# Two edge layers of a graph network: node degrees from the attention layer's ones column, eight row buffers, and PSUM for four and eight groups

## What is computed

```python
x = x + schnet(relu(layernorm(x)), src, dst, edge_weight, edge_attr)   # layer 0
x = x + gat(relu(layernorm(x)), src, dst)                              # layer 1, 8 heads
# layer 2: mean over neighbours
h   = relu(layernorm(x)) @ W + b
agg = segment_sum(h[dst], src);  deg = segment_sum(ones, src)
x   = x + agg * where(deg > 0, 1 / max(deg, 1), 0)[:, None]
# layer 3: two graph convolutions with batch norm; here loops are added once more
deg1 = segment_sum(ones, [dst, loops]);  dinv = rsqrt(deg1)
h = relu(batch_norm(segment_sum(dinv[s] * dinv[d] * (x @ W1)[s], d) + b1))   # 64 wide
z = batch_norm(segment_sum(dinv[s] * dinv[d] * (h @ W2)[s], d) + b2)         # 2 wide
x = x + z @ Wd + bd
```

## Time and profile before

| | |
|---|---|
| timed runs | 6829.5 us median of 3 (6825.88 to 6838.7) |
| profiled execution | 6840.93 us, span of the core 6839.2 us |
| PE / PEld busy | 4606.4 (67%) / 3811.0 us |
| DVE busy | 4114.3 us (60%) |
| POOL busy | 3517.6 us (51%) |
| ACT busy | 1523.6 us (22%) |
| mean granted clock of PE | 0.785 |

### The profile page before, as it was taken

One profiled execution on the slowest core, in us unless ns is written; L12 is line 12 of the kernel. 1 busy time (PEld: TensorE's weight loads), 2 busy tenths in 40 slices (PEclk: granted clock), 3 DMA queues, 4 the chain that ended last, 5 costly groups with the idle time before them and its releaser, 6 DMA issues. The chain is left out here.

```text
span 6839.2 us, 101942 instructions
## 1 busy us (share of the span) xinstructions
PE 4606.4 (67%) x25681; PEld 3811.0 (56%) x25681; DVE 4114.3 (60%) x11101; ACT 1523.6 (22%) x2509; POOL 3517.6 (51%) x3663
## 2 busy tenths in 40 slices
PE   4999999998957777777875666666663333333494
PEld 3777777776747777766764666666642222222231
DVE  3888888887646666666676555555553333333473
ACT  2666566554211111111122000000020000000272
POOL 1566666664055555555612666666615666666202
PEclk8999999999967877878877777777785555555596
DMA  4333333332333333333333222222232111111143
GB/s 146 105 91 90 89 90 90 91 90 75 108 86 84 83 79 81 83 79 82 85 90 119 85 85 85 85 85 86 86 91 47 22 22 22 22 22 22 35 114 106
DMA packets 417562, 537.32 MB, mean 79 GB/s; under 512 B 200349, under 2 KB 289577, under 8 KB 417353
## 3 DMA queue, kind: packets, MB, share of 16 engines
q0 software_dynamic: 154912, 381.74, 20.5%
q1 hardware_dynamic: 262442, 152.99, 8.4%
HBM read 482.43 MB, written 58.81 MB: 79 GB/s over the span
## 5 line engine op out<-in xcount | busy, mean ns | idle before, releaser
L489 POOL DMA_INDIRECT l_rows<-tmp_tab,l_idx x2496 | 2457.1, 984 | 1361.7 <-issue 712.7
L1919 PE MATMUL l_psa<-l_sel,l_rows 128*128 128x128 f32 (+1 forms) x4992 | 1093.5, 371 | 1314.5 <-DVE l_sel L507 1088.1
L1919 PEld LDWEIGHTS l_psa<-l_sel,l_rows 128*128 128x128 f32 (+1 forms) x4992 | 928.7, 244 | 1428.4 <-issue 803.7
L1886 DVE TENSOR_TENSOR acc<-acc,l_psa 128x256 f32 (+1 forms) x1664 | 584.0, 351 | 1193.1 <-issue 534.6
L1156 POOL DMA_INDIRECT l_rows<-tmp_tab,l_idx x832 | 866.7, 1042 | 586.6 <-PE l_psa L1470 329.7
L791 PE MATMUL l_psw<-l_fw,l_ssp 128*128 128x256 f32 x3328 | 782.4, 389 | 52.7 <-DVE l_msg L691 39.7
L791 PEld LDWEIGHTS l_psw<-l_fw,l_ssp 128*128 128x128 f32 x3328 | 624.7, 193 | 224.3 <-issue 73.2
L1470 PE MATMUL l_psa<-l_sel,l_rows 128*128 128x128 f32 x3328 | 627.2, 318 | 81.9 <-DVE acc L1358 43.2
L1358 DVE TENSOR_TENSOR acc<-acc,l_psa 128x384 f32 x832 | 460.8, 554 | 306.5 <-remote 96.2
L1470 PEld LDWEIGHTS l_psa<-l_sel,l_rows 128*128 128x128 f32 x3328 | 524.6, 224 | 106.1 <-DVE acc L1358 56.2
L507 DVE TENSOR_SCALAR l_sel<-iota,rel 128x128 f32<-128x128 f32 x1664 | 387.2, 295 | 193.7 <-issue 147.2
(11 more groups left out here) (313 smaller groups left out, 6243.3 us busy)
## 6 DMA issues: line engine op xcount, KB each, us to landing
l_rows<-tmp_tab,l_idx POOLq DMA_INDIRECT x3328
l_edge<-in_edge_t SPq DMA_DIRECT2D x104, 256.0 KB
tmp_x<-n_X SPq DMA_DIRECT2D x39, 512.0 KB
n_X<-in_x SPq DMA_DIRECT2D x26, 512.0 KB
tmp_tab<-n_O POOLq DMA_DIRECT2D x26, 512.0 KB
l_win<-tmp_att_tab SPq DMA_DIRECT2D x832, 8.0 KB
n_X<-tmp_x SPq DMA_DIRECT2D x26, 512.0 KB
l_lo_b<-tmp_lo_row SPq DMA_DIRECT2D x52, 256.0 KB
```

The costliest lines, as they stand in the source:

```text
L489: nc.gpsimd.indirect_dma_start(out=rows[b][:, t, :], out_offset=None, in_=table[:, :], in_offset=bass.IndirectOffsetOnAxis(ap=idx[q][:, j: ...
L1886: nc.vector.tensor_tensor(a, a, p, ALU.add).then_inc(added, 1)
L1919: last = nc.tensor.matmul(psa[0:n, col:col + P], rows[b][:, t, f:f + n], sel[b][:, t, :], start=True, stop=True)
```

## The change

The kernel after it differs in these places:

- l1: `wx` has a 17th column for each tile, which is one everywhere, so that row 16 of the third plane of `acc` counts the edges of each node. SP writes that row to memory at the start of n2.
- l2 and l3 have eight `rows` and `sel` buffers and four index buffers. PSUM holds `deep` groups, four in l2 and eight in l3, and DVE adds group g - LAG behind the selections of g, LAG being 3 and 7. PE and DVE loop over eight groups a turn, POOL over sixteen.
- l2: no ones product and no `deg` adds. ACT clears `acc`, DVE no longer. What n3 did first with the degrees stands here: the load at SP, the root at ACT, `degrees()` at DVE behind the third selection, and PE's products ahead of its loop, with the 64-wide copy of `dinv_c` replaced by a broadcast operand. The copies go to `dinv_r`, 64 partitions; `deg` is gone.
- n3 has only its staging, transposes and residuals.
- l3: the work for `split` stands behind the seventh selection, and the work after the loop ahead of the last seven adds.

```diff
@@ gather_all
         for b in range(NB):
+            r = (q * NB + b) % len(rows)
             hold(pool, ph, used, (it * NB + b) * per + per)
             if b == NB - 1 and more:
-                indices(it + 1, 1 - q)
+                indices(it + 1, (q + 1) % len(idx))
             for t in range(GT):
                 j = b * GT + t
                 nc.gpsimd.indirect_dma_start(
-                    out=rows[b][:, t, :], out_offset=None, in_=table[:, :],
+                    out=rows[r][:, t, :], out_offset=None, in_=table[:, :],
...
-    with pool.Fori(0, ITERS // 2 - 1) as pair:
-        for q in range(2):
-            tiles(pair * 2 + q, q, True)
+    with pool.Fori(0, ITERS // turns - 1) as turn:
+        for q in range(turns):
+            tiles(turn * turns + q, q, True)
@@ edges_gat
     W2 = 2 * HEADS
+    WC = W2 + 1
...
+                for w in wx:
+                    last = nc.vector.memset(by_edge(w)[:, :, W2:WC], 1.0)
...
-                            left = rows[c.r][:, j, k * P:(k + 1) * P] if k < KH else wx[c.p][:, j * W2:j * W2 + P]
+                            left = rows[c.r][:, j, k * P:(k + 1) * P] if k < KH else wx[c.p][:, j * WC:j * WC + P]
@@ nodes_gat, SP
+                sp.dma_start(dram["deg_row"][:, :], acc[W2:W2 + 1, KH, 0:NP]).then_inc(deg_out, 16)
@@ edges_rows
-def edges_rows(nc, dram, sh, tag, table, width, acc, count=None, split=None):
+def edges_rows(nc, dram, sh, tag, table, width, acc, deep, degree=None, split=None):
...
+    LAG = deep - 1
-        rows = [ph.sb(f"rows{i}", [P, GT, width]) for i in range(NB)]
-        idx = [ph.sb(f"idx{i}", [P, SEG], I32) for i in range(2)]
-        sel = [ph.sb(f"sel{i}", [P, GT, P]) for i in range(NB)]
+        rows = [ph.sb(f"rows{i}", [P, GT, width]) for i in range(ROWS)]
+        idx = [ph.sb(f"idx{i}", [P, SEG], I32) for i in range(4)]
+        sel = [ph.sb(f"sel{i}", [P, GT, P]) for i in range(ROWS)]
-        psa = ph.ps("psa", 2 * GT * wide)
-        psc = ph.ps("psc", 2 * GT * P)
+        psa = ph.ps("psa", deep * GT * wide)
...
+                @block.scalar
+                def _(act):
+                    for k in range(KH):
+                        last = nc.scalar.activation(acc[:, k, :], sh["iota"][:, 0:1].to_broadcast([P, NW]), ACT.Copy)
+                    last.then_inc(acc_zero, 1)
+                    act.wait_ge(deg_in, 16)
+                    nc.scalar.activation(dinv_c[:, :], deg_c[:, :], ACT.Sqrt, bias=sh["ones"][:, 0:1]).then_inc(rooted, 1)
+                    for c in range(CHUNKS):
+                        act.wait_ge(spread, c + 1)
+                        nc.scalar.activation(dinv_r[:, c * CN:(c + 1) * CN], psa[0:H3, (1 + c % 2) * CN:(2 + c % 2) * CN],
+                                             ACT.Copy).then_inc(roots, 1)
...
+                for b in range(ROWS):
+                    select(0, b)
+                    if b == LAG - 1:
+                        if degree:
+                            degrees()
+                        if split:
+                            bytes_of_sources()
+                    if b >= LAG:
+                        add(b - LAG, b - LAG)
+                with dve.Fori(1, GROUPS // ROWS) as turn:
+                    for b in range(ROWS):
+                        select(turn, b)
+                        add(turn * ROWS + (b - LAG), b - LAG + (ROWS if b < LAG else 0))
+                if split:
+                    same_destination()
+                for g in range(GROUPS - LAG, GROUPS):
+                    add(g, g % ROWS)
...
-                with pe.Fori(0, ITERS) as it:
-                    for b in range(NB):
+                with pe.Fori(0, GROUPS // ROWS) as turn:
+                    for b in range(ROWS):
...
-                            if count is not None:
-                                col = ((b % 2) * GT + t) * P
-                                last = nc.tensor.matmul(psc[:, col:col + P], sh["ones"][:, :], sel[b][:, t, :],
@@ bass_gnn_stack
-                    edges_rows(nc, dram, sh, "l2", dram["tab2"], D, acc, deg)
+                    edges_rows(nc, dram, sh, "l2", dram["tab2"], D, acc, 4, degree=(dinv_r, inv, last_edge, has, dinv_c))
-                edges_rows(nc, dram, sh, "l3", dram["tab3"], H3, acc3, split=(keep_on, one_dst, cont))
+                edges_rows(nc, dram, sh, "l3", dram["tab3"], H3, acc3, 8, split=(keep_on, one_dst, cont))
```

More of the change, by code:

```diff
@@ L1804, in edges_rows @@
             cleared_l, dst_in, linked = ph.sem("cleared_l"), ph.sem("dst_in"), ph.sem("linked")
-        psa = ph.ps("psa", 2 * GT * wide)
-        psc = ph.ps("psc", 2 * GT * P)
+        if degree:
+            dinv_r, inv, last_edge, has, dinv_c = degree
+            deg_c = ph.sb("deg_c", [P, NT])
+            upto, upper, ends = ph.sb("upto", [P, P]), ph.sb("upper", [P, NT]), ph.sb("ends", [P, NT])
+            deg_in, acc_zero, cols_done, cols_in = ph.sem("deg_in"), ph.sem("acc_zero"), ph.sem("cols_done"), ph.sem("cols_in")
+            counted, ranked, rooted, spread, roots = (ph.sem(n) for n in ("counted", "ranked", "rooted", "spread", "roots"))
+        psa = ph.ps("psa", deep * GT * wide)
         S = ph.sem
-        gathered = [S(f"gathered{i}") for i in range(NB)]
+        gathered = [S(f"gathered{i}") for i in range(ROWS)]
         idx_done, sel_done = S("idx_done"), S("sel_done")
-        cleared = S("cleared")
-        win_done = S("win_done", NB)
-        adds = 1 if count is None else 2
-        added = S("added", 2 * GT * adds)
+        win_done = S("win_done", ROWS)
+        added = S("added", deep * GT)
+        by_tile = lambda g: psa[:, g % deep * GT * wide:(g % deep + 1) * GT * wide].rearrange("p (t n) -> p t n", n=wide)
         ph.begin()
@@ L1842, in _ @@
                                              ).then_inc(dst_in, 16)
+            if degree:
+                @block.sync
+                def _(sp):
+                    with nc.allow_non_contiguous_dma(reason="one degree for each partition and node tile"):
+                        sp.dma_start(deg_c[:, :], dram["deg_row"].rearrange("a (t p) -> p (a t)", p=P)).then_inc(deg_in, 16)
+                    sp.wait_ge(deg_in, 16)
+                @block.scalar
[9 more added lines that the diff above has]
+                                             ACT.Copy).then_inc(roots, 1)
             @block.gpsimd
@@ L1862, in _, with same_destination @@
                     last.then_inc(cleared_l, 1)
[L1863 to L1898 removed]
+                def same_destination():
                     keep, one, cont = split
@@ L1913, in _ @@
+                with pe.Fori(0, GROUPS // ROWS) as turn:
+                    for b in range(ROWS):
+                        g = turn * ROWS + b
                         pe.wait_ge(sel_done, g + 1)
[L1914 to L1915 removed]
+                        pe.wait_ge(gathered[b], turn * 64 + 64)
+                        pe.wait_ge(added, GT * (g + 1))
                         for t in range(GT):
                             for k, (f, n) in enumerate(blocks):
[L1918 to L1923 removed]
+                                last = nc.tensor.matmul(by_tile(b)[0:n, t, k * P:(k + 1) * P], rows[b][:, t, f:f + n], sel[b][:, t, :],
@@ L1955, in _ @@
                 sp.dma_start(w[:, :, :], by_half(dram["gcn_w1"])).then_inc(w_in, 16)
-                sp.dma_start(dram["deg_row"][:, :], deg[0:1, 0:NP]).then_inc(deg_out, 16)
-                sp.wait_ge(deg_out, 16)
-                with nc.allow_non_contiguous_dma(reason="one degree for each partition and node tile"):
-                    sp.dma_start(deg_c[:, :], dram["deg_row"].rearrange("a (t p) -> p (a t)", p=P)).then_inc(deg_in, 16)
                 def step(at):
```

163 lines of the change are left out of this document (68 added, 95 removed).

## The result

The change makes the kernel a little faster: 6814.9 us median of 20 runs (6781.5 to 6830.4) against 6832.2 us for the kernel before in 20 runs of the same measurement, ratio 0.9966, 95% interval [0.9953, 0.9979]. By the ratio that is 23 us where 90 were forecast: the direction was right, and the size was not. The time lies outside the forecast's own range of 6700 to 6790, though inside the wide one of 6500 to 6820.

The account below looks back on a forecast made before the run. POOL's gathers, 5.03 us a group, were taken as the floor of l2 and l3, 1046 us each; -70 (l2) and -20 (n3) made -90, 6751 us, and 6740 as median of timed runs. Own range 6700 to 6790, wide range 6500 to 6820.

Parts of the forecast that it names:

- crawl: DVE in l3, some 8 us after POOL restarts: single adds 1.8 to 4.7 us apart, some 15 us a group.
- part (3): l2's start and end: POOL's 7 us wait goes, more groups are open at the last gather; net 0, -7 to +20.
- part (5): l3 with PSUM and buffers for eight groups, adds seven groups late: 0 us, bounds -25 and +25.
- part (2): l2 with more PSUM and buffers takes l3's pace, 5.89 us a group, 1225 us against 1294: -70 us.
- the ring: l2: DVE selects and adds for two groups, PE multiplies them; with PSUM for two, neither goes on before the other ends.
- Part (4): n3's prologue: only staging and the load of X stay, 7 us of 26.4: -20 us, or -12.
- Part (6): The ones column: stride 17 for 16, a fill at the attention layer's start, a row sent out during n2: 0 us.
- (A): Rival: l2's and l3's late signals are hidden by depth, both go to POOL's floor: -425, 6405 us; chance 0.22.
- (B): Rival: the longer DVE loop body in l2 and l3 costs a stop each turn of 8 groups: +92, 6921 us; chance 0.11.
- (C): Rival: l2 keeps its pauses and stays at 6.1 us a group, -25; in all -35, 6795 us; chance 0.13.
- (D): Rival: start and drain +20, l3 +25, l2 at -35: in all -10, 6820 us; chance 0.06.
- The rule of the skill: Instructions stream ahead in sequence, so only a taken branch leaving the two pages at hand, a loop's end, should starve DVE.

Follow-up runs that it names:

- e5: Kernel before, unchanged, on a chip with the crawl: to the last add, l2 took 1281 us and l3 1224 us.
- e6: Changed kernel, unchanged, on a chip with the crawl: ratio 0.9955 to the kernel before on that chip.
- e8: Changed kernel cut to the degree change alone (four buffers, PSUM for two groups), chip with the crawl: ratio 0.9940 to the kernel before.
- e1: Changed kernel cut to the degree change alone (four buffers, PSUM for two groups), chip without the crawl: ratio 0.9970 to the kernel before.
- e2: Changed kernel with l2's degree-chain copies over seven PSUM banks instead of two, chip without the crawl: ratio 0.9965 to the kernel before.
- f4: Changed kernel, unchanged, on a chip without the crawl: ratio 0.9958 to the kernel before on that chip.
- g1: Changed kernel with four row and selection buffers and PSUM for four groups in both layers, chip with the crawl: ratio 0.9908 to the kernel before.
- e11: Changed kernel with only one of l3's four gathers a group, chip with the crawl: l3 took 579 us to its last add.
- e4: Changed kernel with a group's four selections in one DVE instruction, chip without the crawl: ratio 1.0065 to the kernel before.

## Why the prediction was wrong

The mechanism of the steady state was right: l2 took l3's crawl, at the pace forecast. The step that failed is the ends of the stages: part (3), "l2's start and end", was summed at net 0 and came to 21 us, and part (5) left l3's drain out of its sum, where it came to 26. With them goes a slip of 14 us in part (2). Point by point:

- *Part (2), l2 at 5.89 us a group, -70.* From POOL's restart at 3780.56 to its last gather, 200 groups took 5.92 us each (4965.0 - 3780.6 over 200), half a percent off. But I set 208 x 5.89 = 1225, which is gathers only, against 1294 us to the last add; gathers against gathers it is 1225 to 1281, -56. Measured -37 for the gathers and -28 to the last add (-36 and -22 between e5 and e6). The part took degrees, PSUM and buffers together as what cuts the ring. Apart, the degrees bring 21 us (e5 to e8) and PSUM 17 to 22 more, with POOL's runs going from 8 to 12 to 16 gathers; the buffers bring nothing to the pace and take 16 to 21 at the end.
- *Part (3), start and end, 0 (-7 to +20).* The start took 58.9 us for eight groups, 11.8 over the pace, because the chain crawls while POOL gathers: I had priced it by n3, where nothing gathers, though the prediction itself had DVE starve while POOL gathers. POOL's wait of 7 us, which was to go, became one of 18.7. The drain is 22.4 us against 13.1. The two make 21 us, just over the upper bound. Together: 1225 + 11.8 + 22.4 + 200 x 0.03 = 1265, the measured 1266.
- *Part (4), n3 -20.* Right: -27 from l2's last add to l3's first gather in this pair, -20 between e5 and e6; the first residual comes 5.1 us after the first issue where 7 were forecast.
- *Part (5), l3 0 (-25 to +25).* Within its bounds, +17: gathers 9 us shorter (1229.3 and 1220.7), drain 26 us longer (9.0 and 34.6), 3.4 of it the work that now lies ahead of the last adds. The drain was named and priced at 19 us, but only as a bound; seven groups of adds had to come after the last gather by the order of the program, so they belonged in the sum. The formula for a run's length uses 3.5 groups in the first 8 us where its sentence says three; with three it gives 18.7 us, not 22.5, and nothing in the sum hangs on it.
- *Part (6), 0.* No run shows a cost.
- *The rivals.* (A) is out on chips with the crawl: from two groups' PSUM to four the pace changes by 0.1 us a group and stays 0.9 over POOL's floor. (B) is out: a turn of DVE's loop is now 32 gathers, and POOL's pauses stand once in 16, as in l3 before. (C) is out by its own sign, l2's pauses for each 8 gathers: they stand once in 16. (D), l3 gives it back and start and drain are dearer, had a chance of 0.06 and comes nearest, 6820 against 6815. Its start and drain (+20) and its l3 (+25) came out as 21 and 17. That the total fits so well is luck: its terms for l2, n3 and l3 add up to -10 where the pair of traces has -28, -27 and +17, or -38, and the 14 us that the attention layer took more there stand in no forecast.
- *The rule of the skill.* In e1 DVE is hardly starved, 9.7 us of gaps under issue in 700, and in e8 it is, with the same program on another chip. So neither the section "Instruction fetch mechanics" of the Trainium skill's page "Runtime: NRT & Kernel Launch" nor my count of instructions tells the whole: the trace before the change was that of one kind of chip.

## What to carry to other kernels

Buffers ahead of a consumer that is slow in the steady state are not free: where the consumer is behind, they are full when the producer ends, and the drain grows with their number (9 to 11 us of l2 with four, 20 to 29 with eight). Where the consumer keeps up, they cost nothing there (9 us in e1, 8 to 9 in e2 and f4). Price the drain in the sum, and look whether fewer buffers with the same PSUM give the same pace (g1: four buffers, 0.9908, against eight, 0.9955, each against the kernel before on its own chip). And a chain of short answers between engines, moved from a quiet stage under a stream of gathers, is not priced by what it took in the quiet.

## What the runs showed of the hardware

- Chips of two kinds: with the same kernel, 5950 us on two chips and 6770 to 6830 on the others. On the slower ones all stages with gathers are longer (the first edge layer's gathers 1481 to 1513 against 1322 to 1323 us, l3's 1207 to 1229 against 1045 to 1055 with four selections a group). In l3 the granted clock is the same in both, 0.50 of full speed, so it isn't what makes l3 longer.
- The crawl goes with gathers by index in close order, not with bytes: none with plain transfers at twice the bytes, none with one gather in 2.6 us (e11).
- A gather beside a DVE operation with two full-width operands in SBUF took up to some 1.4 us instead of 0.95 (e4), in 55 and 114 of 832 gathers over 1.05; with it l2 and l3 were 2 and 4% longer.
- Products of a broadcast column with the identity took twice the PE records of the transposes that they replaced, 104 for 52, and 14.2 us instead of 9.6 (f4).
